# Cross attention: the mask written into the score banks by ScalarE, and both halves of a row of maxima transposed at once

## The reference

```
x = x + self_attention(layernorm(x))        # 8 bit fake-quantized weights and inputs, causal
x = x + cross_attention(layernorm(x), ctx)  # ctx 64 x 120 x 256, mask 64 x 256 x 120 (True: left out)
x = x + layer(layernorm(x))                 # attention, then a mixture of 8 experts, top 2, capacity

cross attention, for each batch and head (256 queries n, 120 keys m, d = 16):
    s = q @ k.T / 4;  s = where(mask, -big, s)
    p = exp(s - max) / (sum over m of exp(s - max) + the extra term of softmax1)
    out = p @ v;  y = concat(heads) @ Wproj + bproj
```

## Time and profile before

| | us |
|---|---|
| median of 3 runs | 5969.68 (5968.39 to 5971.0) |
| profiled execution | 5964.57 |
| its span, first to last instruction | 5962.9 |
| self attention, first to last maxima | 157 to 1171 |
| cross attention, first to last maxima | 1227 to 2402 |
| attention of the last layer, first to last maxima | 2458 to 3892 |
| TensorE busy | 5621.1 |
| VectorE busy | 3721.2 |
| ScalarE busy | 3120.9 |
| GpSimd busy | 2036.6 |

### The profile page before, as it was taken

How to read it: one execution, slowest core, us unless ns; L and a number is a source line. 1 busy time by engine, 2 the same in 40 slices (tenths; PEclk the granted TensorE clock), 3 DMA queues, 4 the chain that set the end, 5 groups by cost and what they waited for, 6 DMA issues and landing times. The chain is left out here.

```text
span 5962.9 us, 144169 instructions
## 1 busy us (share of the span) xinstructions
PE 5621.1 (94%) x44441; PEld 4031.8 (68%) x44441; DVE 3721.2 (62%) x10169; ACT 3120.9 (52%) x6803; POOL 2036.6 (34%) x1753
## 2 busy tenths in 40 slices
PE   0999999989999999799999999958999999999998
PEld 0677777667777777577777777734666666666666
DVE  7888888778888887688888888875111111111111
ACT  4788888746666666477777777635121111211111
POOL 0322222233333333244444444401333333333332
PEclk9999999989999999999999999979999999999999
DMA  5777777556666665466766666631222222222221
GB/s 157 178 184 182 182 185 180 148 159 175 174 173 173 174 174 166 120 178 170 182 171 175 177 170 181 168 26 49 39 53 51 33 49 53 32 45 51 38 39 20
DMA packets 625511, 750.10 MB, mean 126 GB/s; under 512 B 131075, under 2 KB 554188, under 8 KB 625328
## 3 DMA queue, kind: packets, MB, share of 16 engines
q1 hardware_dynamic: 568992, 679.62, 43.7%
q0 software_dynamic: 49152, 63.10, 6.6%
q10 hardware_dynamic: 7184, 5.00, 0.3%
HBM read 476.49 MB, written 272.24 MB: 126 GB/s over the span
## 5 line engine op out<-in xcount | busy, mean ns | idle before, releaser
L1488 ACT ACTIVATE exp_hT<-exp_hid,exp_b 128x512 f32<-128x512 f32 x512 | 351.8, 687 | 1487.3 <-PE exp_hid L1466 1372.3
L1476 PE MATMUL exp_res<-exp_w,exp_hT 128*128 128x256 f32 x4096 | 901.2, 381 | 0.8 <-ACT exp_hT L1488 0.8
L1466 PE MATMUL exp_hid<-exp_xT,exp_w 128*128 128x512 f32 x2048 | 891.0, 593 | 0.9 <-DVE exp_xT L1496 0.9
L1476 PEld LDWEIGHTS exp_res<-exp_w,exp_hT 128*128 128x128 f32 x4096 | 773.8, 190 | 112.2 <-ACT exp_hT L1488 1.6
L1566 POOL DMA_INDIRECT out_dram<-exp_gated,exp_token x256 | 406.1, 1586 | 1099.4 <-issue 412.7
L931 DVE TENSOR_REDUCE F_tops<-F_score 128x2 f32<-128x512 f32 x1024 | 684.3, 686 | 59.8 <-PE F_score L685 40.8
L822 ACT ACTIVATE F_probs<-F_scoreT 128x512 f32<-128x512 f32 x1024 | 583.8, 590 | 236.8 <-PE F_scoreT L654 236.8
L1466 PEld LDWEIGHTS exp_hid<-exp_xT,exp_w 128*128 128x128 f32 x2048 | 389.8, 191 | 464.6 <-issue 458.5
L1496 DVE COPY exp_xT<-exp_turn 128x512 f32<-128x512 f32 x128 | 82.6, 686 | 803.2 <-PE exp_turn L1450 803.2
L931 DVE TENSOR_REDUCE A_tops<-A_score 128x3 f32<-128x384 f32 x1024 | 531.6, 554 | 62.3 <-PE A_score L671 54.0
L1532 DVE SCALAR_TENSOR_TENSOR exp_y<-exp_res,exp_b2s 128x512 f32<-128x512 f32 x128 | 88.5, 692 | 735.4 <-PE exp_res L1476 735.4
(11 more groups left out here) (330 smaller groups left out, 12099.1 us busy)
## 6 DMA issues: line engine op xcount, KB each, us to landing
QS<-d_q SPq DMA_DIRECT2D x384, 192.0 KB, 3.6
KS<-d_k SPq DMA_DIRECT2D x256, 192.0 KB, 4.0
QS<-d_q SPq DMA_DIRECT2D x384, 128.0 KB, 3.9
KS<-d_k SPq DMA_DIRECT2D x256, 128.0 KB, 4.0
d_q<-A_q_parts SPq DMA_DIRECT2D x64, 384.0 KB, 3.6
d_k<-A_k_parts SPq DMA_DIRECT2D x64, 384.0 KB, 3.9
QS<-d_q SPq DMA_DIRECT2D x384, 64.0 KB, 3.7
d_q<-X_q_parts SPq DMA_DIRECT2D x64, 384.0 KB, 4.0
```

The costliest lines, as they stand in the source:

```text
L1466: last = nc.tensor.matmul(h[:, :], w1[k][:, a, f * P:(f + 1) * P], xT[par][:, a, :], start=a == 0, stop=a == 1)
L1476: last = nc.tensor.matmul(res[t][:, s, :], hT[par][:, f, (2 * t + s) * P:(2 * t + s + 1) * P], w2[k][:, f, :], start=f == 0, stop=f == NF - 1)
L1488: nc.scalar.activation(hT[par][:, f, :], hid[f % 2][:, :], ACT.Relu, bias=b1[k][:, f:f + 1])\
```

## The change

- In X, a new step "seed" on ScalarE (one turn ahead, like maxima) copies the mask of the batch, repeated for the two heads, into the score bank. It waits for `score_read` of the bank's last use, seed 0 for `mask_ready` also, and counts `seeded`. TensorE's maxima wait for `seeded` in place of `mask_ready` and `score_read`; the two mask matmuls are gone, and the four products add to what is in the bank (start=False, as before). Once before the loop, TensorE writes all three banks with one matmul each, and ScalarE waits for these (`opened`).
- In all three kinds, `top_parts` has its halves of queries innermost, so that rowsA and rowsB are one transposition to 32 rows of 128 in place of two to 16 rows of 256; `top_rows` is 32 x 128.
- The orders of X on all five engines are rewritten; SHIFTED moves k_rest one turn later (2 in place of 3).

```diff
-        "SP": ("fetch loadB k_store refetch q_store mload rowsB loadA ctxT stats rowsA proj"),
-        "PE": ("v maxima pv3 attend rowsB maxima attend tok0 maxima tok1 attend xT1 maxima ctxT aT attend pv0 yT "
-              "maxima xT0 maxima wo q k attend attend rowsA proj pv1 maxima attend pv2 maxima attend"),
-        "ACT": ("evac3 q_rest rowsB attend attend xT1 ctxT aT yT evac0 xT0 attend attend q k rowsA attend k_rest "
-              "attend evac1 attend evac2 attend"),
-        "DVE": ("topB v maxima maxima mcopy tok0 tok1 norm maxima maxima topA wo maxima stats aggr var maxima c0 "
-              "c1 proj c2 c3 c4 c5 c6 c7 maxima c8 maxima c9 c10 apply"),
-        "POOL": ("fetch q_rest refetch mload q k k_rest"),
+        "SP": ("fetch loadB mload q_store rowsB k_store refetch ctxT stats loadA rowsA proj"),
+        "PE": ("v pv3 maxima attend rowsB maxima tok0 attend tok1 maxima xT0 attend ctxT aT maxima xT1 attend yT "
+              "q maxima maxima wo attend pv0 k attend proj rowsA pv1 maxima attend pv2 maxima attend"),
+        "ACT": ("seed seed q_rest evac3 attend rowsB seed k_rest attend xT0 seed ctxT aT xT1 seed seed yT attend "
+              "q attend seed attend attend evac0 k rowsA evac1 seed attend evac2 attend"),
+        "DVE": ("topB v maxima tok0 tok1 norm maxima maxima maxima maxima topA wo mcopy stats aggr maxima var c0 "
+              "c1 c2 proj c3 c4 c5 maxima c6 c7 c8 maxima c9 c10 apply"),
+        "POOL": ("q_rest k_rest mload fetch q refetch k"),
...
-           "X": {"loadB": 1, "q_store": 2, "q_rest": 2, "k_store": 2},
+           "X": {"loadB": 1, "q_store": 2, "q_rest": 2, "k_store": 2, "k_rest": 2},
...
-        top_parts = [sb(f"top_parts{i}", [P, 2, 2, H // 2], BF16) for i in range(2)]
-        top_rows = [sb(f"top_rows{i}", [H, 256], BF16) for i in range(2)]
+        top_parts = [sb(f"top_parts{i}", [P, 2, H // 2, 2], BF16) for i in range(2)]
+        top_rows = [sb(f"top_rows{i}", [2 * H, P], BF16) for i in range(2)]
...
+                if kind == "X":
+                    for s in score:
+                        mm(s[:, 0:2 * HB * KN], ident_b[:, :], C["wT"][:, 0, :, :].rearrange("p c n -> p (c n)")[:, 0:2 * HB * KN],
+                           start=True, stop=True).then_inc(opened, 1)
...
-                            if i == 0 and kind == "X":
-                                pe.wait_ge(mask_ready, g + 1)
-                            need(pe, score_read, earlier(g, i, SB))
+                            if kind == "X":
+                                pe.wait_ge(seeded, G * g + i + 1)
+                            else:
+                                need(pe, score_read, earlier(g, i, SB))
...
-                                for u in range(HB):
-                                    mm(s[:, 2 * u * KN:2 * (u + 1) * KN].rearrange("p (n k) -> p n k", n=2), ident_b[:, :],
-                                       mask[gp][:, :, 0:KN], start=u == 0,
-                                       stop=False, skip_group_check=True)
...
-                            for j in range(2):
-                                last = nc.tensor.transpose(Wb[0:H, j * P:(j + 1) * P], top_parts["AB".index(name[4])]
-                                                           [:, j, :, :].rearrange("p a h -> p (a h)"), ident_b[:, :])
+                            last = nc.tensor.transpose(Wb[0:2 * H, 0:P], top_parts["AB".index(name[4])][:, :, :, :]
+                                                       .rearrange("p a h j -> p (a h j)"), ident_b[:, :])
...
+                        if name == "seed":
+                            if i == 0:
+                                act.wait_ge(mask_ready, g + 1)
+                            need(act, score_read, earlier(g, i, SB))
+                            nc.scalar.activation(score[i % SB][:, 0:2 * HB * KN].rearrange("p (u n k) -> p u n k", u=HB, n=2),
+                                                 mask[gp][:, :, 0:KN].unsqueeze(1).broadcast_to([P, HB, 2, KN]), ACT.Copy)\
+                                .then_inc(seeded, 1)
...
-                            last = nc.scalar.activation(top_rows[h][:, :], Wb[0:H, 0:256], ACT.Copy)
+                            last = nc.scalar.activation(top_rows[h][:, :], Wb[0:2 * H, 0:P], ACT.Copy)
```

More of the change, by code:

```diff
@@ L376, in attention @@
     for engine, names in SCHEDULE[kind].items():
-        counts = {"attend": 0, "maxima": 0}
+        counts = {"attend": 0, "maxima": 0, "seed": 0}
         STEPS[engine] = []
@@ L390, in earlier @@
         return G * g + i - banks + 1 if i >= banks else G * (g - 1) + (G - 1 - i) // banks * banks + i + 1
-    LAG = {"loadA": 2, "loadB": 2, "mload": 2, "mcopy": 1, "v": 1, "maxima": 1, "topA": 1, "topB": 0, "rowsA": 1, "rowsB": 0,
+    LAG = {"loadA": 2, "loadB": 2, "mload": 2, "mcopy": 1, "v": 1, "maxima": 1, "seed": 1, "topA": 1, "topB": 0, "rowsA": 1, "rowsB": 0,
            "attend": 0, "pv0": 0, "pv1": 0, "pv2": 0, "evac0": 0, "evac1": 0, "evac2": 0,
@@ L501, in attention @@
                 [sb(f"{n}{i}", [P, 2, KP], BF16) for i in range(2)] for n in ("mask", "maskT"))
-            zeroed = sem("zeroed")
+            zeroed, opened, seeded = sem("zeroed"), sem("opened"), sem("seeded")
             y_in, y_ready, ctx_in, mask_in, mask_ready, maskT_ready, xb_ready, x1_out, xres_in, based_ready, mask_zero = (
@@ L814, in _ @@
             def _(act):
+                if kind == "X":
+                    act.wait_ge(opened, SB)
                 for b, par in iterations(act):
                     for name, i, g, gp in steps(b, par, "ACT"):
+                        if name == "seed":
[5 more added lines that the diff above has]
+                                .then_inc(seeded, 1)
                         if name == "attend":
@@ L942, in _ @@
                                 chain.step(nc.vector.tensor_tensor(tops[:, 1, hs], tops[:, 1, hs], tops[:, 2, hs], ALU.max))
-                            chain.step(nc.vector.tensor_copy(top_parts[h][:, :, 0, :], tops[:, 0:2, hs]))
-                            chain.step(nc.vector.tensor_tensor(top_parts[h][:, :, 1, :], tops[:, 0:2, hs], top_parts[h][:, :, 0, :],
-                                                               ALU.subtract))
+                            leading, rest = (top_parts[h][:, a, :, :].rearrange("p h j -> p j h") for a in range(2))
+                            chain.step(nc.vector.tensor_copy(leading, tops[:, 0:2, hs]))
+                            chain.step(nc.vector.tensor_tensor(rest, tops[:, 0:2, hs], leading, ALU.subtract))
                         if name == "norm" and kind == "A":
```

## The result

The changed kernel takes 5942.41 us (median; 5936.58 to 5949.17), the kernel before 5969.68. The ratio is 0.9954, with a 95% interval of 0.9942 to 0.9966: faster by 27 us, where 114 were forecast. The profiled execution has a span of 5942.2 us (5962.9 before).

The account below looks back on a forecast made before the run. TensorE was taken to bound the kernel: a cross attention turn of 18.40 - 1.68 - 0.12 + 0.15 = 16.75 us, 102 us over 62 turns, plus 12 us elsewhere, 114 in all, gives 5856 us. Range for 8 in 10: 5822 to 5905.

Parts of the forecast that it names:

- What bounds the kernel before: All three attention stages: TensorE, over 99% busy, sets the turn; 18.40 us a turn in cross attention.
- Part 1: TensorE in cross attention: sixteen mask matmuls a turn removed, 0.21 us a step, 1.68 us off the turn.
- the allowance: Cross attention's new order: 0.15 us a turn charged for near ties such as rowsB waiting for topB (0 to 0.5).
- Part 2: ScalarE in cross attention: eight seeds a turn at 0.49 us, 3.92 us, bringing ScalarE to 15.05 us a turn.
- the rival of a dearer seed: ScalarE's seed copy costs twice the row's price, 0.98 us: 0.5 us more a turn, 6000 us; chance 4%.
- Part 3: rowsA and rowsB, all three stages: one transposition in place of two saves 0.12 us a turn.
- Part 4: New order on every queue in cross attention: nearly all steps have slack; 0.15 us a turn charged.
- The landing of loadA: Its six loads land a microsecond or so before the next turn's first maxima step: closer than before, still hidden.
- the rival on ScalarE: ScalarE's order and waits take back half the gain: turn 17.55 us, 5905 us; chance 20%.
- The rival on VectorE: VectorE becomes the bound if the order doubles its small steps' time lost beside GpSimd: turn 17.4, 5896 us; chance 12%.
- the case of no change: The seeds' waits give back what the matmuls took, time within 12 us of before; chance 2%.

Follow-up runs that it names:

- e14: e11 with the mask matmuls back on TensorE and no seeds: 5931.32 us.
- e4: The kernel before with the single transposition of the maxima rows alone: 5955.75 us.
- e2: The changed kernel with every GpSimd addition and subtraction in cross attention (X) on 8 columns, so values differ: 5857.14 us.
- e3: The changed kernel with seeds of 8 columns in place of 484, so the maxima leave the mask out: 5911.92 us.
- e12: e11 with the 8-column seeds of e3, maxima without the mask: 5880.38 us.
- e7: The changed kernel's new orders and single transposition, but with the mask matmuls kept on TensorE and no seeds: 5961.79 us.
- e11: The changed kernel with GpSimd's q_rest waiting for topB, q for topA and xb for norm, and fetch ahead of mload: 5880.32 us.
- e9: The changed kernel with GpSimd's q_rest subtraction waiting for topB, q's for topA, and fetch ahead of mload: 5894.6 us.
- e8: The changed kernel with rowsB two places later in TensorE's order: 5946.15 us.
- e5: The changed kernel with GpSimd's subtractions for q and k and the sum xb in X cut in four pieces each, no waits: 5896.60 us.
- e10: The changed kernel with twelve unread 128-column matmuls on TensorE ahead of its wait for topB at rowsB: 5936.63 us.

## Why the prediction was wrong, point by point

- **What bounds the kernel before.** Right that TensorE did, but the base of the sum was off twice. The stretch of 736 us has 318 of the maxima reductions, 8 a turn, so it holds 39.75 turns and not 40: a turn is 18.52 us, not 18.40. And its busy share hid something: the earlier trace rows has TensorE at over 99%, and still the turn with the matmuls is 18.03 in e14, in another order and with GpSimd clear, where the kernel before with a single transposition has 18.435 (e4). Of these 0.4 us a turn only 0.1 are gaps between matmuls in e4; the rest counts as busy. I took the turn of 18.40 as all work.
- **Part 1, 1.68 us.** Too high: from e14's 18.03 to e2's 16.84 or the shortest turns' 16.62 are 1.2 to 1.4 us, 0.15 to 0.18 a step instead of 0.21. This and the point before offset each other, by luck: 16.60 for a free turn before the allowance, 16.62 the shortest seen.
- **Part 2, 0.49 us a seed.** Right. ScalarE's timeline of the changed kernel has two seeds in 1.07 us and the next step 0.99 behind the first's start:

```profile
1814.96 1.07 ACT L823 ACTIVATE X_score<-X_mask 128x484 f32<-128x484 bf16 x2
1815.95 0.60 ACT L863 ACTIVATE X_yT<-X_work 128x512 bf16<-128x512 bf16 x1
```

  From a seed's start to the next operation's it is 0.495 us in the median; one by itself takes 573 ns. ScalarE's busy time is 835.37/1025 of 18.40, 15.0 us a turn, with 15.05 forecast. The longest seed is 587 ns, so the rival of a dearer seed didn't come about.
- **Part 3.** Right in A and F, 11 us of 12, and near in X, 0.09 us a turn of 0.12; the whole is 14 us in e4, where the sum had 19; the copy of a row of maxima takes 262 ns where the earlier trace rows has 0.36.
- **Part 4, the step that failed.** I gave VectorE 2.4 to 2.7 us for the chain from maxima 7 to topB, against 2.6 on TensorE, and charged 0.15 us a turn. For topB I used 2 x 0.175 to 2 x 0.32, the shortest and the mean. The earlier trace rows had its maximum beside it, 1281 ns. A mean of 315 made of 175 and 1281 is no delay of 0.14 each time but one of 1.1 in one of eight; with one such hit the chain is 3.5 us long and TensorE waits 0.9, and 1.08 is what the timeline shows. In place of 0.15 us a turn TensorE's gaps are 0.94, with up to 0.46 more for the clock, and the turn of 18.40 lies 1.6 to 1.8 us over the free ones (16.84 in the mean of e2, 16.62 the shortest). And I took the frequency as given, though part 4 rewrites the very orders that decide which of VectorE's steps meets GpSimd: the subtraction's mean went from 352 to 595 ns, L108's from 960 to 179. The prediction had the sign for this ("if TensorE waited at rowsB for the maxima's parts"), without a price for it.
- **The landing of loadA, and the rival on ScalarE, 20%.** Two rows of the changed kernel's waits, 1400 to 2136 us (us in total, times, longest):

```profile
PEld X_score L681 <- ACT X_score L823: 41.3, 80, 1.0
...
PE X_score L681 <- DMA KS<-d_k: 6.1, 17, 0.6
```

  The last load of K holds TensorE for 6.1 us in 40 turns. That is small, but it was forecast as hidden, and it is 0.15 us a turn, by itself as much as the whole allowance. The rival named waits on ScalarE that would take back the half, to 5905. Waits on seeds are there (first row), for weight loads that come ahead of their matmuls; the gaps between matmuls that end with a seed are 1.7 us in 1025. With the hits in place less work on ScalarE gave 30 us (e3), but e12 shows the seeds without price once VectorE is on time.
- **The rival on VectorE, 12%.** The right engines and the right rows, with the wrong condition and price. I made it hang on VectorE's busy time, to be doubled by the new order. The time lost beside GpSimd did not double, it fell from 1.89 to 1.67 us a turn, and VectorE was busy for 80% in the changed kernel; what counted was that 1.1 us fell on one step of a chain for which TensorE waits. The loss grows with the gain (e7 to e14 30 us, changed kernel to e11 62). My reading of that, which no run isolates: in the kernel before, VectorE had 3.4 us a turn in which to make such a delay good, and as TensorE's turn shrinks, the same delay is uncovered.
- **The Trainium skill** says, on its page "SBUF — State Buffer", Who interferes with whom, that VectorE and GpSimd share one port pair as an exclusive lock for a whole instruction, and that tensor_reduce on trn2 never contends. The traces agree on both: the L954 shown above lasts 1.16 us beside an operation of GpSimd of 1.15, and none of the 512 reductions of X is longer than 667 ns. I had drawn from this that the rival could come only through small steps, and read small as cheap. Nor was it small steps alone: in e9 norm's first step, on 512 elements, was held from 0.48 to 1.34 us.
- **TensorE's clock** was in no part of the sum. The earlier trace rows show 1.00 throughout, with no gap of over 0.45 us in the kernel before. In the changed kernel it was a second price of a wait of about a microsecond on this engine, though not of each: e8 has 14 waits of over 0.9 us and one fall.

The result of 5942 lies outside 5822 to 5905. Only the case of no change (2%, within 12 us) had a turn near 18.4, and the measured gain is 27 us. What remains open is the 0.6 us a turn of e11 over the shortest turns, and how the clock's share divides from that of the waits which set it off.

## What to carry to other kernels

Before work is taken off the full engine, list for each step that it waits for the shortest and the longest duration in the trace, not the mean: a small step with 175 and 1281 ns is one that a neighbour can block, and its cover goes with the work that is taken away. Place GpSimd's long two-input operations beside VectorE's reductions, hold them back with a wait until the critical small steps are through, or cut them in pieces; here holding back was worth 62 us on top of the change's 27, and cutting 46. And when a new order is tried, a gain that fails to come need not mean that the order or the moved work is wrong: look for which steps the old collisions have moved to.

## What the runs showed of the hardware

- A VectorE step on 2 or 16 numbers a partition that takes 160 to 180 ns alone takes 1.0 to 1.3 us if GpSimd has just begun an addition or subtraction of 512 float32; one of 512 float32 elements (norm's first step) took 1.34 us instead of 0.48. With GpSimd's operations cut in four (0.28 to 0.56 us each) the steps on 16 numbers took 0.48 us at most (e5, 1265 to 2290 us), at 145 us more busy time of GpSimd in 1025.
- TensorE's granted clock fell from 2.4 to 1.2 GHz for 3.4 us 15 times in 1025 us of the changed kernel, each time behind a wait in which its matmuls had stood for 0.7 to 1.4 us. In e8, with 14 such waits of 0.9 to 1.08 us, it fell once, and in e10, where twelve small matmuls filled the idle time, not at all.
- ScalarE writes 484 float32 elements to a bank, from a bf16 source that is repeated by a zero stride, in 573 ns, 495 from its start to the next operation's, beside 0.60 and 0.49 us for a copy of 512 elements from a bank: no extra cost of the repetition or of the destination shows.
